# Correlation products on 8 x 16 pixel tiles instead of 4 x 32 row strips, with a re-laid copy of the stationary operand

## The chip, the cores and the metric

The kernel runs on one core of one Trainium2 chip. The metric is the device time of one execution in microseconds (us), which covers the profiled span and a little around it. Lower is better.

## The reference

Input is `x` of shape 8 x 512 x 32 x 32 in float32. Two layers follow each other, each `x = x + conv(group_norm(x))`. What is inside `conv`, cut to its core:

```python
norm = sqrt(sum(feature * feature, axis=1));  fn = feature / max(norm, 1e-12)
fp = pad(fn, 2 pixels on each side of h and w)
for cc in range(5):
    for r in range(5):
        sims.append(sum(fp[:, :, r:h + r, cc:w + cc] * fn, axis=1))   # 25 correlation maps
out = relu(einsum('bihw,oi->bohw', concat([feature, vol]), conv_w) + conv_b)
```

So each pixel needs the dot product over 512 channels of its own vector with those of its 5 x 5 neighbours, scaled by the two norms, and then a 1 x 1 convolution from 512 + 25 to 512 channels.

## The kernel before

The work is cut into 16 *units*, one for each layer and image, in teams of four images: units 0 to 3 are layer 0 of images 0 to 3, units 4 to 7 are layer 1 of the same images, and so on. A unit is 512 channels (4 tiles `t` of 128 partitions) by 1024 pixels.

- **Normalising.** VectorE reads each tile for its statistics (L759) and closes them (`stats_done`, last instruction L772). TensorE averages over groups with one small matmul (`average`, L461), VectorE forms scale and offset (`unit_affine`, L778 to L802), and ScalarE writes the normalised tile as float16 high part (`norm_tile`, L627) and twice the float32 value (`double_tile`, L633, GpSimd L432 for units 0 to 2). VectorE's `low_tile` (L808) forms the float16 low part from both. `opnd` holds high and low parts of four units in a ring.
- **Correlation products** (`product`, L470). The pixels are cut into 8 blocks of 4 rows x 32 columns (128 pixels). For each block the stationary operand is the high part of its 128 pixels, and the moving operand is the block's rows with two rows more above and below: 8 x 32 = 256 columns, or 6 x 32 = 192 for the first and last block. There are two moving parts (high, low) and four channel tiles, so a unit has 8 x 4 x 2 = 64 such matmuls. A pair of blocks fills one PSUM bank. There are four pairs `p`; pair `p` waits until ScalarE has copied pair `p - 2` out (`band_out_of_psum`, L643).
- **Skewing.** SyncE writes `band` to DRAM (L340) and reads it back along a diagonal into `skew` (L346), so that each pixel has its neighbours at fixed places. VectorE scales them (`neighbours`, L832 to L852), TensorE transposes them (`turn`, L520), ScalarE copies them to `rows` (L654), and SyncE writes them out (L356, L358). They come back as shifted views: issued by GpSimd (`views_from_dram`, L267 to L277), by SyncE in units 0 and 1. VectorE forms the 25 maps (`correlation`, L817 to L825), and GpSimd's DMAs bring them into `vol` (`volume_in`, L286).
- **Convolution.** A unit has 8 groups (4 output tiles x 2 pixel halves). Each is 12 matmuls of 512 columns (`channels`, L530) and one with `vol` (`volume`, L539). ScalarE applies relu (`rectified`, L662), VectorE adds into `x` (`added`, L886).

The order on every engine is written by hand. Units 0 to 2 have their own start-up sequence. From `k = 3` on there are equal *slots*: in slot `k` TensorE runs `products(k, 0..3)` with `average(k + 1)` between pair 1 and pair 2, then groups 4 to 7 of unit `k - 2`, groups 0 and 1 of unit `k - 1`, `turn(k)`, and groups 2 and 3 of unit `k - 1`. VectorE does in slot `k`: `unit_affine(k + 1)`, `correlation(k - 1)`, `low_tile(k + 1, 0)` and `(.., 1)`, `added` of group 4, `low_tile(.., 2)`, `added`, `neighbours(k)`, `low_tile(.., 3)`, and then additions and statistics of unit `k + 2`. Slot 4 also turns the weights of layer 1 (L510, L874).

## Time and profile before

| | |
|---|---|
| median of 3 runs | 540.35 us (539.79 to 542.28) |
| profiled execution | 540.12 us |
| its span | 538.4 us |
| TensorE matmul busy | 490.8 us, 91% |
| VectorE busy | 350.5 us, 65% |
| ScalarE busy | 278.6 us, 52% |
| GpSimd busy | 131.8 us, 24% |

The span is what the profiler records from the first to the last instruction; the profiled execution's own time is 1.7 us longer. TensorE's share covers work with different limits: in the start-up TensorE waits for the other engines, later it does not. So the stretches have to be read apart.

### The profile page before, as it was taken

The numbers are of one execution on the slowest core, as the hardware profiler recorded it, in microseconds if no ns is written. First come the engines' busy times: TensorE is split into PE (matmuls) and PEld (weight loads), VectorE is DVE, ScalarE is ACT, GpSimd is POOL, SyncE is SP. The second block draws the span as 40 slices with busy tenths as digits, with TensorE's granted clock in tenths as the row PEclk, the third lists the DMA queues.
The fourth block names the chain that finished last, engine by engine and source line by source line (L and its number), as shares of the span: only waits on it lengthen the run. The fifth ranks groups of instructions, "written<-read, shape, count | busy, mean of one in ns | idle before, by whom it ended". The sixth has DMA issues, their size and how long they took to land.

```text
span 538.4 us, 7705 instructions
## 1 busy us (share of the span) xinstructions
PE 490.8 (91%) x2824; PEld 278.2 (52%) x2824; DVE 350.5 (65%) x820; ACT 278.6 (52%) x370; POOL 131.8 (24%) x189
## 2 busy tenths in 40 slices
PE   0658699489998999999999999999999999999996
PEld 0535355354644646464645556464646455564442
DVE  4788794767869296958758595858677676433322
ACT  1352544575394656647393757556473938433222
POOL 3453511040521313131220404040313112040400
PEclk9989799789999999999999999999999999999999
DMA  8282444441332716494957625042332326362332
GB/s 295 99 270 67 129 165 133 133 134 38 94 92 74 219 49 211 149 309 131 321 165 254 212 102 161 15 129 47 98 89 75 110 79 185 138 203 90 126 126 114
DMA packets 58547, 75.81 MB, mean 141 GB/s; under 512 B 11764, under 2 KB 45612, under 8 KB 58510
## 3 DMA queue, kind: packets, MB, share of 16 engines
q1 hardware_dynamic: 48718, 66.40, 36.7%
q0 software_dynamic: 9792, 8.92, 7.0%
q8 instruction: 22, 0.36, 0.3%
q14 instruction: 15, 0.12, 0.1%
HBM read 34.97 MB, written 37.79 MB: 135 GB/s over the span
## 4 chain that ended last, share of the span: by engine, by line
PE 77%; DVE 10%; ACT 4%; DMA 4%; POOL 2%; SPq 2%; issue 2%; DVEq 0%; ACTq 0%
PE conv_ps L530 56%; PE gram_ps L470 14%; PE conv_ps L539 5%; DVE stats L759 3%; POOL v L432 2%; DVE opnd L808 2%; DMA xs<-in_x_dram 1%; ACT opnd L627 1%; PE turn_ps L520 1%; ACT v L633 1%; DVE wmax L858 1%; ACT act_out L662 1%; DMA skew<-band_dram 1%; DMA band_dram<-band 1%; DVE xs L886 1%
## 5 line engine op out<-in xcount | busy, mean ns | idle before, releaser
L530 PE MATMUL conv_ps<-opnd,wh 128*128 128x512 f16 x512 | 194.9, 381 | 1.2 <-DVE wl L874 1.2
L530 PE MATMUL conv_ps<-opnd,whh 128*128 128x512 f16 x512 | 194.7, 380 | 0.0
L530 PE MATMUL conv_ps<-opnd,wl 128*128 128x512 f16 x512 | 194.7, 380 | 0.0
L662 ACT ACTIVATE act_out<-conv_ps,bias,wdown 128x512 f32<-128x512 f32 x128 | 96.4, 775 | 141.0 <-PE conv_ps L539 129.1
L886 DVE TENSOR_TENSOR xs<-xs,act_out 128x512 f32<-128x512 f32 x128 | 87.7, 696 | 50.8 <-ACT act_out L662 50.2
L470 PE MATMUL gram_ps<-opnd 128*128 128x256 f16 (+1 forms) x960 | 105.0, 269 | 3.4 <-ACT band L643 3.4
L470 PEld LDWEIGHTS gram_ps<-opnd 128*128 128x128 f16 x960 | 91.1, 100 | 16.6 <-ACT band L643 3.7
L808 DVE SCALAR_TENSOR_TENSOR opnd<-opnd,v 128x1024 f16<-128x1024 f16 x64 | 78.4, 1235 | 28.7 <-ACT v L633 21.3
L627 ACT ACTIVATE opnd<-xs,affine 128x1024 f16<-128x1024 f32 x64 | 78.8, 1238 | 17.4 <-DVE affine L802 17.4
L759 DVE BATCH_NORM_STATS2 stats<-xs 128x6 f32<-128x512 f32 x128 | 79.9, 681 | 5.6 <-DMA xs<-in_x_dram 5.6
L530 PEld LDWEIGHTS conv_ps<-opnd,whh 128*128 128x128 f16 x512 | 50.0, 98 | 61.2 <-issue 1.0
L530 PEld LDWEIGHTS conv_ps<-opnd,wh 128*128 128x128 f16 x512 | 50.2, 98 | 58.8 <-POOL whh L424 1.3
L530 PEld LDWEIGHTS conv_ps<-opnd,wl 128*128 128x128 f16 x512 | 50.2, 98 | 57.5 <-issue 0.8
L633 ACT ACTIVATE v<-xs,affine 128x1024 f32<-128x1024 f32 x52 | 64.4, 1238 | 6.1 <-DVE opnd L808 6.1
L267 POOL DMA_DIRECT2D mirror<-rows_dram x14 | 9.5, 678 | 232.0 <-DMA rows_dram<-rows 232.0
L286 POOL DMA_DIRECT2D vol<-corr_h x48 | 33.2, 697 | 105.7 <-DVE corr_h L825 105.6
L539 PE MATMUL conv_ps<-vol,wvol 96*128 96x512 f16 x128 | 47.2, 396 | 11.7 <-DMA vol<-corr_h 11.7
L643 ACT ACTIVATE band<-gram_ps 128x448 f32<-128x448 f32 (+1 forms) x60 | 32.5, 560 | 20.2 <-PE gram_ps L470 20.2
L817 DVE TENSOR_TENSOR mirror<-mirror,rn_own 100x256 f32<-100x256 f32 x16 | 6.8, 424 | 49.1 <-DMA rn_far<-rows_dram 49.1
L277 POOL DMA_DIRECT2D rn_far<-rows_dram x56 | 34.1, 744 | 0.0
L539 PEld LDWEIGHTS conv_ps<-vol,wvol 96*128 96x128 f16 x128 | 12.6, 100 | 27.6 <-DMA vol<-corr_h 12.3
L432 POOL TENSOR_SCALAR v<-xs,affine 128x1024 f32<-128x1024 f32 x12 | 21.7, 1817 | 18.5 <-DVE affine L802 11.8
(77 smaller groups left out, 238.6 us busy)
## 6 DMA issues: line engine op xcount, KB each, us to landing
xs<-in_x_dram SPq DMA_DIRECT2D x32, 512.0 KB, 6.4
band_dram<-band SPq DMA_DIRECT2D x64, 256.0 KB, 2.9
out_dram<-xs SPq DMA_DIRECT2D x32, 512.0 KB, 2.9
skew<-band_dram SPq DMA_DIRECT2D x32, 266.0 KB, 3.5
vol<-corr_h POOLq DMA_DIRECT2D x48, 50.0 KB, 2.7
rows_dram<-rows SPq DMA_DIRECT2D x32, 65.8 KB
rows_dram<-rows SPq DMA_DIRECT2D x32, 63.3 KB
mirror<-rows_dram POOLq DMA_DIRECT2D x14, 110.9 KB, 2.6
```

Source lines behind the costliest of these rows:

```text
L277: eng.dma_start(rn_far[c:QPARTS:QUARTERS, 0:run], bass.AP(rows_dram, rn_row + c * QRUN, [[1, S], [PW, S], [1, run]])).then_inc(arrived, 16)
L286: eng.dma_start(vol[at:at + NS, k % 2, :].rearrange("s (q n) -> s q n", q=QUARTERS), corr_h[:, part, :]).then_inc(vol_in, 16)
L470: return pe.matmul(gram_at(u, p)[:, at:at + (r1 - r0) * WI], opnd[:, u % RING, 0, t, j * P:(j + 1) * P], opnd[:, u % RING, part, t, r0 * W ...
L530: pe.matmul(conv_ps[:, g % 4, :], w[:, l, t, m * P:(m + 1) * P], opnd[:, u % RING, part, t, n * HALF:(n + 1) * HALF], start=(t == 0 and w ...
L539: pe.matmul(conv_ps[:, g % 4, :], wvol[0:96, l, m * P:(m + 1) * P], vol[0:96, u % 2, n * HALF:(n + 1) * HALF], start=False, stop=True).the ...
L627: act.activation(opnd[:, u % RING, 0, t, :], xs[:, ring_slot(unit_batch(u)), t, :], ACT.Identity, bias=affine[:, 0, 1, t:t + 1], scale=aff ...
L633: act.activation(v2[:, t % 2, :], xs[:, ring_slot(unit_batch(u)), t, :], ACT.Identity, bias=affine[:, 1, 1, t:t + 1], scale=affine[:, 1, 0 ...
L643: act.activation(band[:, p, a:z], gram_at(u, p)[:, a:z], ACT.Copy).then_inc(band_sb, 1)
L662: act.activation(act_out[:, g % 2, :], conv_ps[:, g % 4, :], ACT.Relu, bias=bias[:, l, m:m + 1], scale=wdown[:, l, m:m + 1]).then_inc(relu, 1)
L759: last = dve.bn_stats(stats[:, t, h, :], xs[:, ring_slot(b), t, h * HALF:(h + 1) * HALF])
L808: dve.scalar_tensor_tensor(out=opnd[:, u % RING, 1, t, :], in0=opnd[:, u % RING, 0, t, :], scalar=-2.0, in1=v2[:, t % 2, :], op0=ALU.mult, ...
L886: dve.tensor_tensor(xt, xt, act_out[:, g % 2, :], ALU.add).then_inc(x_sum, 1)
```

## The change

The pixels are cut into 8 tiles of 8 rows x 16 columns (still 128 pixels). With the border of two pixels a tile needs 12 x 20 neighbours. Of these only what lies inside the image is computed: 18 of the 20 columns (`HELD = TC + R`), and 12 rows, or 10 for the top and bottom tiles. The moving operand is therefore 12 x 18 = 216 or 10 x 18 = 180 columns, read as runs of 18 elements out of rows of 32. [...] `strips` has room for one unit only: a copy waits until all products of the unit before are done. ScalarE's copy out of PSUM, the DRAM layout of `band` and the diagonal read follow the new tile shape (the read takes runs of 85 elements in place of 133). `turn` writes each transposed tile to its place in the image, as 8 runs of 16 columns in PSUM. Four small DMAs at the start (`pads`) go, and the clearing of `band` on GpSimd grows from 2 x 64 to 1920 columns. In the slots VectorE's order changes: `low_tile` and `strip_tile` of tiles 0 and 1 come ahead of `correlation(k - 1)`.

```diff
+    TR, TC = 8, 16
+    DOWN, ACROSS = HI // TR, WI // TC
+    BR, BC = TR + 2 * R, TC + 2 * R
+    BAND = BR * BC
+    HELD = TC + R
+        strips = sb("strips", [P, KT, ACROSS, HI * TC], F16)
...
-            def product(u, j, t, part):
-                return pe.matmul(gram_at(u, p)[:, at:at + (r1 - r0) * WI],
-                                 opnd[:, u % RING, 0, t, j * P:(j + 1) * P],
-                                 opnd[:, u % RING, part, t, r0 * WI:r1 * WI],
+            def product(u, p, c, t, part):
+                r0, r1 = held_rows(p)
+                c0 = 0 if c == 0 else WI - HELD
+                at = c * HALF // 2
+                return pe.matmul(gram_at(u, p)[:, at:at + HELD * (r1 - r0)],
+                                 strips[:, t, c, p * P:(p + 1) * P],
+                                 image(opnd[:, u % RING, part, t, :])[:, r0:r1, c0:c0 + HELD],
...
                 if p == 0:
                     pe.wait_ge(high, KT * (u + 1))
                     pe.wait_ge(low, KT * (u + 1))
+                    pe.wait_ge(stripped, KT * (u + 1))
...
+            def strip_tile(u, t):
+                wait(dve, gram, PAIRS * u)
+                dve.wait_ge(high, KT * u + t + 1)
+                dve.tensor_copy(strips[:, t, :, :].rearrange("p c (h w) -> p c h w", w=TC),
+                                opnd[:, u % RING, 0, t, :].rearrange("p (h c w) -> p c h w", c=ACROSS, w=TC)
+                                ).then_inc(stripped, 1)
...
             for t in range(KT):
+                strip_tile(0, t)
                 low_tile(0, t)
...
                 low_tile(3, 3)
+            for t in range(KT):
+                strip_tile(3, t)
...
             for k in range(STEADY, SLOTS):
+                if valid(k + 1):
+                    for t in range(2):
+                        low_tile(k + 1, t)
+                        strip_tile(k + 1, t)
                 if valid(k - 1):
                     correlation(k - 1)
-                if valid(k + 1):
-                    low_tile(k + 1, 0)
-                    low_tile(k + 1, 1)
...
+                        for t in {1: (2,), 3: (3,)}.get(j, ()):
+                            strip_tile(k + 1, t)
...
-                    last = pe.transpose(turn_ps[0:H_PART + NROWS, 0, i * P:(i + 1) * P],
+                    at = i % ACROSS * TC
+                    last = pe.transpose(image(turn_ps[0:H_PART + NROWS, 0, :])[:, i // ACROSS * TR:(i // ACROSS + 1) * TR,
+                                                                              at:at + TC],
```

TensorE, the products of one unit in a slot, before (rows of 128 stationary columns by so many moving columns; L461 is `average`):

```order
L470 MATMUL gram_ps<-opnd 128x192 x8
L470 MATMUL gram_ps<-opnd 128x256 x24
L461 MATMUL turn_ps<-mv,avg 128x8
L470 MATMUL gram_ps<-opnd 128x256 x24
L470 MATMUL gram_ps<-opnd 128x192 x8
```

And after, at the same place:

```order
L469 MATMUL gram_ps<-opnd,strips 128x180 x16
L469 MATMUL gram_ps<-opnd,strips 128x216 x16
L461 MATMUL turn_ps<-mv,avg 128x8
L469 MATMUL gram_ps<-opnd,strips 128x216 x16
L469 MATMUL gram_ps<-opnd,strips 128x180 x16
```

The number of matmuls is the same, 64; each streams fewer columns.

VectorE, a slot from the end of `unit_affine` to the start of `neighbours`, before (L817 to L825 are `correlation`, L808 is `low_tile`, L886 `added`):

```order
L802 TENSOR_SCALAR affine<-affine 128x8
L817 TENSOR_TENSOR mirror<-mirror,rn_own 100x8x32
L818 TENSOR_TENSOR own<-own,rn_far 100x8x32
L820 TENSOR_TENSOR corr<-own,mirror 100x256
L823 TENSOR_SCALAR corr_h<-corr 100x256
L825 SCALAR_TENSOR_TENSOR corr_h<-corr,corr_h 100x256
L808 SCALAR_TENSOR_TENSOR opnd<-opnd,v 128x1024 x2
L886 TENSOR_TENSOR xs<-xs,act_out 128x512
L808 SCALAR_TENSOR_TENSOR opnd<-opnd,v 128x1024
L886 TENSOR_TENSOR xs<-xs,act_out 128x512
L832 TENSOR_SCALAR nsq<-skew 128x8
```

And after (L832 to L840 are now `correlation`, L815 `low_tile`, L901 `added`, L822 the new copy):

```order
L815 SCALAR_TENSOR_TENSOR opnd<-opnd,v 128x1024
L822 COPY strips<-opnd 128x1024
L815 SCALAR_TENSOR_TENSOR opnd<-opnd,v 128x1024
L822 COPY strips<-opnd 128x1024
L832 TENSOR_TENSOR mirror<-mirror,rn_own 100x8x32
L833 TENSOR_TENSOR own<-own,rn_far 100x8x32
L835 TENSOR_TENSOR corr<-own,mirror 100x256
L838 TENSOR_SCALAR corr_h<-corr 100x256
L840 SCALAR_TENSOR_TENSOR corr_h<-corr,corr_h 100x256
L901 TENSOR_TENSOR xs<-xs,act_out 128x512
L815 SCALAR_TENSOR_TENSOR opnd<-opnd,v 128x1024
L822 COPY strips<-opnd 128x1024
```

`correlation` has moved behind two `low_tile` and two copies, and three copies stand ahead of `neighbours`. The fourth copy comes after `low_tile(.., 3)`.

## Rows read from the trace of the kernel before

**Rows 1.** The page: busy us, share of the span and instructions of each engine.

```profile
PE 490.8 (91%) x2824; PEld 278.2 (52%) x2824; DVE 350.5 (65%) x820; ACT 278.6 (52%) x370; POOL 131.8 (24%) x189
```

**Rows 2.** Busy time by stretch: start-up, slots 3 and 4, the rest.

```profile
core 0: us, PE busy (x) PEld busy (x) DVE busy (x) ACT busy (x) POOL busy (x), PEclk, DMA share, GB/s
61.77:110.59 48.82, 39.44 (x216) 22.38 (x216) 36.23 (x80) 25.23 (x33) 9.30 (x8) 0.87 0.45 139
110.59:163.38 52.79, 49.61 (x278) 27.88 (x279) 38.66 (x89) 32.31 (x42) 17.03 (x25) 0.97 0.32 90
163.38:538.40 375.02, 370.32 (x2124) 204.85 (x2124) 231.34 (x547) 200.26 (x265) 77.42 (x122) 1.00 0.45 143
```

**Rows 3.** One slot, same columns.

```profile
322.25:351.86 29.61, 29.61 (x175) 16.75 (x174) 21.85 (x57) 17.61 (x23) 6.35 (x10) 1.00 0.30 84
```

**Rows 4.** Products of one unit alone (L470): 8 of 192 columns, 24 of 256.

```profile
322.25:322.91 0.66, 0.66 (x9) 0.66 (x8) 1.00 0.00 0
322.91:325.53 2.62, 2.62 (x26) 2.24 (x24) 1.00 0.41 82
```

**Rows 5.** TensorE's timeline: start us, us, engine, line, operation.

```profile
11.78 0.57 PE L461 MATMUL turn_ps<-mv,avg 128*128 128x8 f32 x2 [11.78 <-DVE mv L772]
...
101.84 1.89 PE L539 MATMUL conv_ps<-vol,wvol 96*128 96x512 f16 x4 [7.00 <-DMA vol<-corr_h]
...
110.59 5.12 PE L470 MATMUL gram_ps<-opnd 128*128 128x256 f16 x32 [2.19 <-ACT band L643]
...
163.38 0.63 PE L510 MATMUL gram_ps<-ident,xs 128*128 128x128 f32 x4 [2.01 <-DVE wl L874]
...
325.53 0.29 PE L461 MATMUL turn_ps<-mv,avg 128*128 128x8 f32 x2
...
345.37 0.60 PE L539 MATMUL conv_ps<-vol,wvol 96*128 96x512 f16 x2
345.80 0.60 PE L520 MATMUL turn_ps<-ident,nbr 128*115 128x128 f32 x4
```

**Rows 6.** VectorE groups by form: mean ns of one behind the busy time.

```profile
L808 DVE SCALAR_TENSOR_TENSOR opnd<-opnd,v 128x1024 f16<-128x1024 f16 x64 | 78.4, 1235 | 28.7 <-ACT v L633 21.3 <-POOL v L432 7.2
...
L817 DVE TENSOR_TENSOR mirror<-mirror,rn_own 100x256 f32<-100x256 f32 x16 | 6.8, 424 | 49.1 <-DMA rn_far<-rows_dram 49.1
...
L823 DVE TENSOR_SCALAR corr_h<-corr 100x256 f16<-100x256 f32 x16 | 4.7, 294 | 0.6
...
L886 DVE TENSOR_TENSOR xs<-xs,act_out 128x512 f32<-128x512 f32 x128 | 87.7, 696 | 50.8 <-ACT act_out L662 50.2
```

**Rows 7.** VectorE's timeline in the slot from 322.25.

```profile
329.32 0.43 DVE L817 TENSOR_TENSOR mirror<-mirror,rn_own 100x256 f32<-100x256 f32 x1 [1.06 <-DMA rn_far<-rows_dram]
...
330.90 0.43 DVE L825 SCALAR_TENSOR_TENSOR corr_h<-corr,corr_h 100x256 f16<-100x256 f32 x1
...
333.95 1.22 DVE L808 SCALAR_TENSOR_TENSOR opnd<-opnd,v 128x1024 f16<-128x1024 f16 x1 [1.04 <-ACT v L633]
...
338.76 0.17 DVE L832 TENSOR_SCALAR nsq<-skew 128x8 f32<-128x8 f32 x1
339.85 0.20 DVE L835 RECIPROCAL rn<-nrm 128x8 f32<-128x8 f32 x1 [0.91 <-ACT nrm L648]
...
341.72 1.21 DVE L808 SCALAR_TENSOR_TENSOR opnd<-opnd,v 128x1024 f16<-128x1024 f16 x1
...
351.44 0.16 DVE L772 TENSOR_TENSOR mv<-mv,gtmp 128x4 f32<-128x4 f32 x1
```

**Rows 8.** VectorE's and ScalarE's timeline at unit 3.

```profile
101.06 1.23 DVE L808 SCALAR_TENSOR_TENSOR opnd<-opnd,v 128x1024 f16<-128x1024 f16 x1 [1.04 <-ACT v L633]
102.20 4.84 DVE L759 BATCH_NORM_STATS2 stats<-xs 128x6 f32<-128x512 f32 x8
...
108.66 1.45 ACT L662 ACTIVATE act_out<-conv_ps,bias,wdown 128x512 f32<-128x512 f32 x2 [3.43 <-DVE xs L886]
```

**Rows 9.** The page: DMA issues (times issued, KB each, median us to landing).

```profile
vol<-corr_h POOLq DMA_DIRECT2D x48, 50.0 KB, 2.7
```

More of the change, by code:

```diff
@@ L479, in first_products @@
                     pe.wait_ge(high, t + 1)
+                    pe.wait_ge(stripped, t + 1)
                     pe.wait_ge(low, t + 1)
                     for p in range(PAIRS):
-                        for j in (2 * p, 2 * p + 1):
+                        for c in range(ACROSS):
                             for part in range(2):
-                                last = product(0, j, t, part)
+                                last = product(0, p, c, t, part)
                         if t == KT - 1:
@@ L492, in products @@
                     pe.wait_ge(low, KT * (u + 1))
+                    pe.wait_ge(stripped, KT * (u + 1))
                 pe.wait_ge(band_sb, PAIRS * u + p - 1)
-                for j in (2 * p, 2 * p + 1):
+                for c in range(ACROSS):
                     for t in range(KT):
                         for part in range(2):
-                            last = product(u, j, t, part)
+                            last = product(u, p, c, t, part)
                 last.then_inc(gram, 1)
```

71 lines of the change are left out of this document (35 added, 36 removed).

## The prediction, written before the changed kernel ran

> **What bounds the kernel now.** First the page's head: TensorE is busy for 490.8 of 538.4 us [rows 1]. That share hides two regimes, so I read the busy time by stretch next. From 163.38 us to the end TensorE is busy for 370.3 of 375.0 us [rows 2], and in a slot for all 29.61 us, with VectorE at 21.9 and ScalarE at 17.6 [rows 3]. There a microsecond less of matmuls is a microsecond less of time, as long as no other engine's order becomes longer than the slot. Before that TensorE has holes. Its timeline shows which waits end last: the first statistics at 11.78, `vol` of unit 1 at 101.84 (7.00 us of waiting), ScalarE's `band` at 110.59 (2.19), VectorE's `wl` at 163.38 (2.01) [rows 5]. Ahead of each of these VectorE, ScalarE and SyncE set the pace, and shorter products only make the hole longer.
>
> **The products.** A unit has 48 matmuls of 256 columns and 16 of 192. The distance from start to start is what counts: the first eight take 0.66 us, 82.5 ns each for 192 columns; the next 24 take 2.62 us, 109.2 ns each for 256 [rows 4]. That is 0.417 ns a column plus 2.5 ns, at full granted clock. After, a unit has 32 of 216 and 32 of 180. By that line they take 92.5 and 77.5 ns. Sum: 6.56 us before, 32 x 92.5 + 32 x 77.5 = 5.44 after, so 1.12 us less per unit. Two reservations. The shortest distance that the trace shows is 82.5 ns, and there the weight loads already fill the time (0.66 of 0.66 us); if that is a floor, the saving is 0.96. And the moving operand is now read in runs of 18 elements, which no row shows; a read that is no slower costs nothing, and one at half speed would add 5.4 us per unit. I take 1.12: VectorE reads runs of 32 out of rows of 36 (L817, `mirror`, 424 ns for 256 elements) at the rate at which it reads whole runs (L886: 696 ns for 512, so 1.06 ns an element and 152 ns fixed, which gives 424 for 256) [rows 6], so breaks between runs alone cost nothing there. Units 5 to 15, eleven of them, lie wholly where TensorE is the bound: 11 x 1.12 = 12.3 us. For units 0, 1, 2 and 4 the shorter products end in front of a wait, so I count nothing. Of unit 3 the second half (5.12 us for 32 matmuls after the wait at 110.59, partly at the low clock: the stretch has 0.87 on average before it [rows 2, 5]) shrinks by a sixth, 0.8 us.
>
> **The copy.** Four per unit, 64 in all, 1024 float16 elements. No row shows one. Bounds: `low_tile` handles 1024 elements with two inputs in 1235 ns. `corr_h` (L823), one input, takes 294 ns for 256: with 152 fixed that is 0.555 ns an element, about half of the two-input form's 1.06, and by it the copy takes 720 ns. That row reads four bytes an element and the copy two; if speed goes by bytes it is 152 + 0.277 x 1024 = 436 ns, the low end [rows 6]. I take 0.44 us, since both sides of the copy are half as wide and its runs of 16 are even. The Trainium skill, "VectorE: DVE Perf Modes", section on the perf-mode tier table, says a one-input copy with 16-bit data on both sides in SBUF runs four elements at a time, and with mixed or 32-bit data two; L823 at half the cost per element of L817 agrees with the second half, and no row shows the first. The sum does not use it.
>
> **A slot after the change.** Times from the slot's start T (322.25 before). `average` came at T + 3.28 [rows 5]; it comes at T + 2.72 now, 0.56 earlier, and ScalarE's chain of norm and double tiles with it. `low_tile(.., 1)` started at T + 11.70, when ScalarE's `v` landed [rows 7], so now at 11.14; the first copy fits in the hole of 1.04 us ahead of it. It ends at 12.36, the second copy at 12.8, `correlation` (329.32 to 331.33, 2.0 us) at 14.8 [rows 7]. It used to lie in a hole of VectorE that ScalarE left; now it does not. Then addition, low tile, addition (0.70, 1.23, 0.70 by their rows [rows 6], less some overlap between neighbours) to 17.2, third copy 17.6. `neighbours` took 2.96 us (338.76 to 341.72) with 0.91 of waiting for ScalarE, which by then stands free: 2.4, so to 20.0. `turn` stands at T + 23.55 - 1.12 = 22.4 on TensorE [rows 5]: not late. Then the 9.88 us from the start of the last low tile (341.72) to the end of `stats_done` (351.60, L772) [rows 7] and the fourth copy in them: 20.0 + 9.88 + 0.44 = 30.3. The slot is now 28.49 long and the next `average` can run at 28.49 + 2.72 = 31.2. So 0.9 us are left, of 3.5 before (351.60 against 351.86 + 3.28 = 355.14). Three copies lie on this path; the point at which VectorE becomes the bound is 0.44 + 0.9 / 3 = 0.74 us for a copy. `vol` is the other queue that gets later: `correlation` ends at 14.8, GpSimd starts some 0.7 later, issues three DMAs of about 0.7 each, and the last lands 2.7 after [rows 9], so 20.3; the first `volume` stood at T + 23.1 [rows 5] and stands at 22.0: 1.7 us are left of some 9.
>
> **Start-up.** GpSimd's longer clearing and the `pads` that go lie under the first load and its statistics, for which TensorE waits until 11.78 [rows 5]: nothing. Units 0 and 1: the copy ahead of `low_tile(u, 0)` is not covered, the other three fall into waits for GpSimd's `v`: 2 x 0.4. Unit 2: three copies in a dense stretch make `average(3)` some 2 us late, but the chain of SyncE's issues (views, band, skew) from `turn(1)` on ends only some 0.5 us later, so I estimate that 0.5 of all this remain at the last low tile of unit 3. Unit 3: all four copies stand between that tile (101.06) and the statistics (102.20), whose end frees the additions, on which ScalarE waits for 3.43 us (108.66) [rows 8], then `band`, then TensorE (110.59) [rows 5]: 4 x 0.44 = 1.8 on the path. Together +2.2 at 110.59, minus the 0.8 above: +1.4 at the start of slot 4. Slot 4: TensorE waits for `wl`, behind `neighbours` in VectorE's order. By the walk above, with statistics of the slot's own (scaling of layer 1's maxima ahead), `correlation` and copies leave `wl` 1.3 later. +2.7 at 163.38.
>
> **The sum.** 540.1 (the profiled execution, which is 0.2 under the median of 540.35) + 2.7 - 12.3 = 530.5; I say 531. ScalarE's copies are shorter (432 or 360 columns for 512 or 448) and the diagonal read carries less, in shorter pieces: beside other work, nothing, within 0.5 us either way in the start-up.
>
> **Rivals.**
> (A, forecast) 531, own range 527 to 535: the floor of 82.5 ns takes 1.8 off, a copy of 0.72 us adds 4 x 0.28 + 3 x 0.28 = 2.0 in the start-up and nothing in slots, and a start-up kinder than I walked it gives 2.7 back.
> (B) One of the thin margins in the slot breaks (0.9 us to `average`, 1.7 to `vol`), or `turn` gets slower: 0.5 us in each of 11 slots, 536. For it: both margins are estimates, and slots with image loads have slower landings (the trace's `vol` at 101.84 came late). Against: the margins are positive in every slot that I walked. A rule speaks for the `turn` part: four transposes stand 0.11 us apart, 0.44 together, and were they to take double, 11 x 0.44 = 4.8 would give 535. The Trainium skill, "PSUM — Partial Sum Buffer", section on the specifications, says any non-contiguous pattern in PSUM slows matmuls significantly; the trace has no such write, and the runs are of 16 float32.
> (C) The copy runs at one element a cycle, like `low_tile`, 1.23 us. The slot's VectorE path grows by 3 x 0.8 = 2.4 us and passes the margin by 1.5 (it decides from 0.74 us a copy), and the slot becomes 28.49 + 1.5 = 30.0 in place of 29.61: 11 x 0.4 = 4 to 5 more than before, and the start-up costs 2.7 + 7 x 0.8 = 8.3, with some 2 for unit 2. 540 + 5 + 10 = 555 or so. Slower than before. Against: L823 is faster than that per element already.
> (D) Broken runs slow the moving operand. A unit reads 16 x 44 = 704 runs; at 1.12 / 704 = 1.6 ns a run (four columns' time) the gain is gone, and at half speed it is 540.1 + 2.7 + 11 x (5.4 - 1.1) = 590. Slower too. Nothing in the trace shows it on TensorE.
> (E) No change, 538 to 542: any of these by half.
>
> **Chances.** A 0.65, B 0.13, C 0.08, D 0.08, E 0.06. What a measurement can tell from no change is about 0.5%, 2.7 us. Faster: A and most of B, 0.75. Same: E and the rest of B, 0.09. Slower: C and D, 0.16. Range 526 to 541: C and D stay outside, with 0.03 below.
>
> **What would show it.** Products: 216-column matmuls 92.5 ns apart, a unit in 5.44 us, slots of 28.5 us with TensorE busy throughout. Copy: L822 at 0.42 to 0.46 us. The end of `stats_done` some 0.9 us ahead of `average`, no wait of TensorE at L461 in the slots. `vol` landing ahead of the volume matmul. Start-up: the wait for `band` ends at about 112.8, the one for `wl` at about 166. Wrong it would be if the product distance doesn't follow the columns, or if TensorE waits at L461, at the volume or at `turn` in each slot.

## The result, and the profile after

| | before | after |
|---|---|---|
| time, median | 539.99 us (538.54 to 542.28) | 544.19 us (540.38 to 547.7) |
| profiled execution | 540.12 us, span 538.4 | 546.94 us, span 545.2 |
| TensorE busy | 490.8 us, 91% | 485.6 us, 89% |
| VectorE busy | 350.5 us, 65% | 373.2 us, 68% |

The changed kernel takes 1.0073 times as long, 95% interval 1.0055 to 1.0091. The prediction said 531, in a range of 526 to 541, and gave 0.16 to slower. It was wrong, in the sign too. In the comparisons by stretch below the profiled execution of the kernel after is one of its longer ones (546.94 us in a spread of 540.38 to 547.7), so what it loses is somewhat more than the medians' 4.2 us.

One word on what is new on VectorE, since its times are read below: the copy `strip_tile` (L822) lays the high part of one channel tile into `strips`, first the left half of the image and then the right one, so that the 128 pixels of a tile lie together.

First the busy time by stretch, cut where TensorE's waits end, as [rows 2] were (the row of 391.85 is one late slot, for [rows 3]); columns as there.

```profile
core 0: us, PE busy (x) PEld busy (x) DVE busy (x) ACT busy (x) POOL busy (x), PEclk, DMA share, GB/s
64.08:117.21 53.13, 40.03 (x217) 22.92 (x217) 37.49 (x87) 24.61 (x33) 9.89 (x12) 0.82 0.42 126
117.21:169.72 52.51, 48.02 (x278) 27.41 (x279) 40.45 (x96) 32.04 (x42) 13.60 (x19) 0.96 0.27 72
169.72:302.71 132.99, 129.54 (x752) 71.47 (x753) 95.17 (x229) 74.56 (x100) 27.71 (x42) 0.98 0.51 166
302.71:545.20 242.49, 235.57 (x1373) 128.63 (x1371) 150.14 (x360) 122.94 (x165) 52.17 (x80) 1.00 0.38 118
391.85:420.61 28.76, 28.76 (x175) 16.25 (x174) 22.07 (x55) 17.40 (x23) 6.59 (x10) 1.00 0.28 77
```

The late slot does what was forecast: 28.76 us against 29.61, TensorE busy all through. The loss lies ahead of such slots. The end of the start-up came at 163.38 [rows 5] and comes at 169.72, 6.3 us later. By comparing the starts of equal slots: slot 5 begins 9.3 us later than before, slot 10 (322.25 in [rows 3]) 11.35 later at 333.60, the last one 7.8 later (478.14 for 470.35). So everything up to slot 5 cost 9.3 us, the five slots in the middle 2 more in place of gaining, and only the slots after that gained. Of the 9.3, 3.0 lie behind the end of the wait, and they are the granted clock: from there to slot 5 TensorE has no further wait, and the same work takes 13.49 us at a mean granted clock of 0.78, where the kernel before took 10.52 (163.38 to 173.90) at 1.00.

```profile
169.72:183.21 13.49, 13.48 (x56) 6.64 (x57) 9.94 (x18) 4.74 (x8) 1.25 (x2) 0.78 0.13 45
```

The products follow the columns. TensorE's timeline of the late slot (start, duration, engine, line, operation) shows the 64 products of the unit. Each row of 32 names only its first form; it holds 16 of 180 and 16 of 216 columns, in the order shown with the change:

```profile
391.85 2.92 PE L469 MATMUL gram_ps<-opnd,strips 128*128 128x180 f16 x32
394.61 0.30 PE L461 MATMUL turn_ps<-mv,avg 128*128 128x8 f32 x2
394.76 3.10 PE L469 MATMUL gram_ps<-opnd,strips 128*128 128x216 f16 x32
397.70 0.38 PE L533 MATMUL conv_ps<-opnd,wh 128*128 128x512 f16 x1
```

From start to start they are about 79 and 93.5 ns apart (77.5 and 92.5 forecast). The convolution follows at 397.70, 5.85 us after the first product.

The waits of SyncE, by line: in total, times, longest. First before, then after.

```profile
SPq L346 <- DMA band_dram<-band: 38.1, 16, 3.6
```

```profile
SPq L358 <- ACT rows L661: 100.7, 12, 12.6
SPq L342 <- ACT band L650: 98.2, 41, 17.6
SPq L325 <- DVE xs L901: 95.8, 24, 8.3
SPq L348 <- DMA band_dram<-band: 79.4, 16, 8.1
```

SyncE waits 79.4 us, in place of 38.1, until the bands have landed in DRAM, ahead of the diagonal read. What that does is seen at unit 2, before and then after (SyncE's issues of a line, with the time that they take):

```profile
87.24 2.13 SPq L340 DMA_DIRECT2D band_dram<-band  x4
92.06 0.91 SPq L346 DMA_DIRECT2D skew<-band_dram  x2
```

```profile
89.64 3.11 SPq L342 DMA_DIRECT2D band_dram<-band  x4
98.01 0.94 SPq L348 DMA_DIRECT2D skew<-band_dram  x2
```

The writes are issued 2.4 us later than before and the read 5.95 us later. TensorE's timeline shows the rest of the path: `turn` waits for `neighbours`, then the products for a copy, which stands behind these in VectorE's order, then the second half of the products for `band`.

```profile
103.84 1.20 PE L522 MATMUL turn_ps<-ident,nbr 128*115 128x128 f32 x4 [3.22 <-DVE nbr L867]
109.22 5.34 PE L469 MATMUL gram_ps<-opnd,strips 128*128 128x180 f16 x32 [4.18 <-DVE strips L822]
117.21 4.56 PE L469 MATMUL gram_ps<-opnd,strips 128*128 128x216 f16 x32 [2.12 <-ACT band L650]
```

The page's count of packets (the single pieces in which the DMA engines move data), which the first experiment gives its meaning:

```profile
DMA packets 49836, 71.62 MB, mean 131 GB/s; under 512 B 27628, under 2 KB 36900, under 8 KB 49798
```

### The profile page after: what moved, and what is told of

It is laid out like the page before. It is cut to its first block, busy times and chain, and to the rows that moved or that the text cites. A ratio compares the mean times of both kernels' runs of the same rounds, so it can differ in the third digit from the quotient of the medians.

```text
span 545.2 us, 7837 instructions
## 1 busy us (share of the span) xinstructions
PE 485.6 (89%) x2824; PEld 274.2 (50%) x2824; DVE 373.2 (68%) x884; ACT 274.5 (50%) x370; POOL 135.6 (25%) x188
## 2 busy tenths in 40 slices
DMA packets 49836, 71.62 MB, mean 131 GB/s; under 512 B 27628, under 2 KB 36900, under 8 KB 49798
## 4 chain that ended last, share of the span: by engine, by line
PE 45%; DVE 23%; DMA 16%; POOL 5%; ACT 4%; issue 4%; SPq 2%; DVEq 0%; ACTq 0%
PE conv_ps L533 34%; PE gram_ps L469 7%; DVE stats L766 5%; DMA rows_dram<-rows 4%; DMA rn_far<-rows_dram 4%; DVE opnd L815 4%; DVE xs L901 4%; PE conv_ps L542 3%; DMA band_dram<-band 2%; DMA out_dram<-xs 2%; POOL v L432 2%; DVE strips L822 2%; ACT opnd L630 1%; DMA skew<-band_dram 1%; ACT v L636 1%
## 5 line engine op out<-in xcount | busy, mean ns | idle before, releaser
L815 DVE SCALAR_TENSOR_TENSOR opnd<-opnd,v 128x1024 f16<-128x1024 f16 x64 | 78.9, 1233 | 55.8 <-ACT v L636 53.8
L901 DVE TENSOR_TENSOR xs<-xs,act_out 128x512 f32<-128x512 f32 x128 | 87.2, 686 | 36.0 <-ACT act_out L669 35.4
L469 PE MATMUL gram_ps<-opnd,strips 128*128 128x180 f16 (+1 forms) x960 | 93.4, 254 | 8.0 <-DVE strips L822 4.2
L469 PEld LDWEIGHTS gram_ps<-opnd,strips 128*128 128x128 f16 x960 | 85.6, 100 | 15.5 <-ACT band L650 6.9
L295 POOL DMA_DIRECT2D vol<-corr_h x48 | 35.4, 745 | 160.0 <-DVE corr_h L840 159.9
L542 PE MATMUL conv_ps<-vol,wvol 96*128 96x512 f16 x128 | 46.4, 389 | 11.7 <-DMA vol<-corr_h 11.7
L650 ACT ACTIVATE band<-gram_ps 128x360 f32<-128x360 f32 (+1 forms) x60 | 28.5, 493 | 15.8 <-PE gram_ps L469 15.8
L822 DVE COPY strips<-opnd 128x1024 f16<-128x1024 f16 x64 | 30.2, 475 | 3.2 <-ACT opnd L630 3.2
L542 PEld LDWEIGHTS conv_ps<-vol,wvol 96*128 96x128 f16 x128 | 12.2, 99 | 28.3 <-DMA vol<-corr_h 14.0
L432 POOL TENSOR_SCALAR v<-xs,affine 128x1024 f32<-128x1024 f32 x12 | 21.7, 1810 | 18.3 <-DVE affine L809 9.2
```

The source lines that it names most:

```text
L295: eng.dma_start(vol[at:at + NS, k % 2, :].rearrange("s (q n) -> s q n", q=QUARTERS), corr_h[:, part, :]).then_inc(vol_in, 16)
L469: return pe.matmul(gram_at(u, p)[:, at:at + HELD * (r1 - r0)], strips[:, t, c, p * P:(p + 1) * P], image(opnd[:, u % RING, part, t, :])[:, ...
L542: pe.matmul(conv_ps[:, g % 4, :], wvol[0:96, l, m * P:(m + 1) * P], vol[0:96, u % 2, n * HALF:(n + 1) * HALF], start=False, stop=True).the ...
L815: dve.scalar_tensor_tensor(out=opnd[:, u % RING, 1, t, :], in0=opnd[:, u % RING, 0, t, :], scalar=-2.0, in1=v2[:, t % 2, :], op0=ALU.mult, ...
L822: dve.tensor_copy(strips[:, t, :, :].rearrange("p c (h w) -> p c h w", w=TC), opnd[:, u % RING, 0, t, :].rearrange("p (h c w) -> p c h w", ...
L901: dve.tensor_tensor(xt, xt, act_out[:, g % 2, :], ALU.add).then_inc(x_sum, 1)
```

## The experiments

Two theories after the result. W: the band is written with a destination of 8 rows by 16 pixels, this form lands late, and all that follows in SyncE's and VectorE's order is late with it. V: the copies and the new order of VectorE's work (correlation behind two low tiles and copies) make additions, views and outputs late. "Changed" is the kernel after, 544.19 us.

**1. The write in one even step.**

```
-    HL_PITCH = TC * (WL_PITCH + 1) - BC
+    HL_PITCH = TC * WL_PITCH
...
-                                  [[HL_PITCH, TR], [WL_PITCH, TC], [1, ACROSS * BAND]])
+                                  [[WL_PITCH, P], [1, ACROSS * BAND]])
```

(and a floor of 1.0e7 in `nsq`, so that nothing overflows: the neighbours are those of wrong pixels here). Expected:

> The changed kernel with the band written to DRAM at one constant pitch over its 128 pixels (one outer dimension of 128 where it had 8 x 16), same 128 runs of 1920 bytes and the same read. Left out: the neighbours are then those of wrong pixels for all but the first image row of a tile, and the floor under the squared length is raised so that nothing overflows; no instruction goes. Theory W (the write in 8 x 16 form lands late: SyncE waited 79.4 us for it where it was 38.1 before): the wait of SyncE for the band falls to about 40 us, the skew of unit 2 lands 2 to 3 us earlier, time 538 to 541. Theory V (VectorE's longer and reordered path makes additions, output DMAs and views late): the wait for the band may fall, the time stays at 543 to 545.

Measured: 531.98 us (531.01 to 535.77), 0.9859 of before (0.9833 to 0.9885). That is 6 us faster than even theory W had it (538 to 541). SyncE's wait is back, and so are the landings; the page's packets beside them:

```profile
SPq L348 <- DMA band_dram<-band: 40.0, 16, 4.2
```

```profile
DMA packets 50348, 71.62 MB, mean 135 GB/s; under 512 B 28140, under 2 KB 37412, under 8 KB 50310
...
band_dram<-band SPq DMA_DIRECT2D x64, 240.0 KB, 2.9
```

The destinations differ by 4 floats a row of 16 pixels, the bytes are the same, and the even form has 512 packets more, 8 for each of the 64 writes. They are small ones (28140 against 27628 under 512 B; of 4 bytes 7247 against 6735). The times of the single packets say the same: of the band's packets of 1920 bytes at most 11 overlapped at any time in the kernel after, with 8 at once for longer than any other number, and up to 22 with the even write, most often 16 when they were many. So the 8-row form ran on 8 of the 16 DMA engines. The Trainium skill, "DMA: Bandwidth & Descriptors", section "Why a DMA increments its semaphore by 16 and not by 1", has the rule: the number of engines is the largest one up to 16 that divides the outermost dimension on both sides; 8 here, and 16 with 128 outside. The packet counts agree: the section lets each engine in use post an end of its own, which makes 8 fewer for each write.

At unit 2 the diagonal read now follows as before:

```profile
87.60 1.92 SPq L342 DMA_DIRECT2D band_dram<-band  x4
92.65 0.92 SPq L348 DMA_DIRECT2D skew<-band_dram  x2
```

and the first stretch of full rate begins at 164.56, 1.2 us later than before. W holds, and the whole 12 us between the two kernels are in this form of the write.

**2. The correlation back ahead of the low tiles and copies.**

```
                     unit_affine(k + 1)
+                if valid(k - 1):
+                    correlation(k - 1)
                 if valid(k + 1):
                     for t in range(2):
                         low_tile(k + 1, t)
                         strip_tile(k + 1, t)
-                if valid(k - 1):
-                    correlation(k - 1)
```

> The changed kernel with correlation(k - 1) put back ahead of the two low tiles in the slots; copies stay behind the low tiles. Theory V, order part: slots in which nothing lands late get as long as TensorE's work (28.5 to 28.8), the additions of unit k - 2 come about 2 us earlier in each slot, the middle slots lose their waits, 539 to 541. Theory W: no change, 543 to 545. A third possibility: in slots whose views land late the low tiles now wait behind them, and it gets slower, 546.

Measured: 558.22 us (556.97 to 559.15), 14.0 more than changed; ratio 1.0332 (1.031 to 1.0354). Theory V had 539 to 541, W no change; the third possibility named was right in kind (slower, for the low tiles then wait behind the views) but had it at 546. TensorE waits ahead of `turn` 13.3 us (6.8 in the kernel after) and for ScalarE's `act_out` 6.5. In a slot from 283 on, VectorE stands 11.77 us before the correlation, with the low tiles and copies queued behind it:

```profile
295.14 0.42 DVE L832 TENSOR_TENSOR mirror<-mirror,rn_own 100x256 f32<-100x256 f32 x1 [11.77 <-DMA rn_far<-rows_dram]
```

Against V's half on the order: it is what kept the late band from costing more.

**3. Copies alone, in the kernel before.** Four idle copies a unit at the places of the changed kernel, old order and old products:

```
+            def strip_tile(u, t):
+                dve.wait_ge(high, KT * u + t + 1)
+                dve.tensor_copy(strips[:, t, :, :].rearrange("p c (h w) -> p c h w", w=16),
+                                opnd[:, u % RING, 0, t, :].rearrange("p (h c w) -> p c h w", c=2, w=16))
```

> The kernel before with the four copies per unit added on VectorE at the changed kernel's places, into a buffer that nobody reads; products, DMAs and the order of correlation as before. Theory V: the copies alone cost 3 us or more, 543 to 545 (my walk had 4 x 0.44 at unit 3, 0.5 ahead of it and 1.3 in slot 4, of which 0.9 are copies: 3.2). Theory W: under 2 us, since the start-up hides them behind SyncE's chain.

Measured: 544.80 us (543.91 to 548.89), ratio 1.0087 (1.0068 to 1.0107). 4.8 us for 64 copies, with the correlation in its old place: V's range, and over the 2 us that W allowed, so here V was right about the copies. In the profiled execution, the longest of the seven (548.89), slot 5 begins 3.1 us later than before, and slots 5, 9 and 10 take 2.9, 1.6 and 0.6 us more than the 29.61 of a late one, with TensorE waiting for `neighbours` and statistics. In the old order the copies cost in slots too.

**4. The 8-row form in the kernel before.**

```
-                                  [[BAND, P], [P * BAND, 2], [1, BAND]])
+                                  [[16 * BAND, 8], [BAND, 16], [P * BAND, 2], [1, BAND]])
```

> The kernel before with the destination pattern of the band write in 8 x 16 form in place of 128, same addresses and the same 256 runs of 1024 bytes. Theory W: the write lands about 2.5 us later each time (SyncE's wait for it 38 to about 80 us), the chain of unit 2 lengthens by as much, 542 to 544. If instead the far spread of the runs in DRAM makes the changed kernel's write slow: no difference, 540.

Measured: 539.82 us, ratio 0.9996 (0.9979 to 1.0012), SyncE's wait 39.2. Inconclusive on W: here 8 steps of 16 pixels are one even step again, and the trace has as many 4-byte packets (7251) as the kernel before, and as many of the band's packets at once (22, 23 before), so the write never was on 8 engines. The rival in the text above, the wide spread of the changed kernel's runs in DRAM, falls by experiment 1, whose runs lie as far apart.

**5. The even write, without the copies.**

```
-                                  strips[:, t, c, p * P:(p + 1) * P],
+                                  opnd[:, u % RING, 0, t, (2 * p + c) * P:(2 * p + c + 1) * P],
...
-                dve.tensor_copy(strips[:, t, :, :]...
+                return
```

> The changed kernel with the band written in one even step over 128 partitions (as in the earlier run of that kind), and now also without the copies of the high parts: the products take blocks of 128 pixels that lie together in the operand as the stationary side. It leaves the copies out, and the products and what follows are of the wrong pixels. Against the 531.98 us of the run with the even write alone it gives the price of the copies. The prediction put them at 0.44 us a tile on VectorE: 4 tiles of unit 3 on the way to the first full-rate slot, 1.8 us, and 1.3 us in slot 4, nothing later. Theory W: the copies cost what was predicted, 2 to 4 us, so 528 to 530 us. Theory V: they also cost in the middle slots, where VectorE is the engine that is late, as four idle copies a unit did in the kernel before (4.8 us), so 525 to 527.5 us. If they are wholly covered: 531 to 532.5.

Measured: 527.76 us (525.99 to 528.27), ratio 0.9767 (0.9746 to 0.9788). The copies cost 4.2 us, between the two theories' ranges; the forecast's terms for them are 1.8 at unit 3 and 1.3 in slot 4, 3.1 together. TensorE's wait for `wl` ends at 160.26 in place of 164.56: all 4.3 us are in the start-up, nothing in the slots after (the last slot begins at 458.44 in place of 462.72).

**6. The even write, with the correlation first.** Edit 1 and edit 2 together.

> The changed kernel with the band written in one even step over 128 partitions, and the correlation of the unit before moved back ahead of the low tiles and the copies of a slot, where the kernel before had it. The products then wait for copies that come at the end of a slot's work on VectorE. Its neighbours are of the wrong pixels, as in the earlier run with the even write. With the late write the same move cost 14 us (558.22 against 544.19). If the cost is that the copies come late for the products whatever the write does: 540 to 548 us. If it came only together with the late band: 531 to 535 us. If the old order is better once the band lands in time: 526 to 530 us.

Measured: 539.36 us (538.01 to 541.33), ratio 0.9991 (0.9976 to 1.0007), just under the first of the three ranges. The old order costs 7.4 us also with a band that lands in time, and 14.0 with the late one. The waits are not for the copies, as that text had it: from 176 us on TensorE waits ahead of `turn` (3.2 us) and `average` (2.7), in slots 5, 6, 8, 9 and 10. So once the copies are there the new order is worth something by itself, and the late band doubles it.

**7. Tiles of 16 rows by 8 columns.** A kernel that computes everything and whose write has 16 outer steps. Pairs are the two edge tiles or the two middle tiles of a half.

```
-    TR, TC = 8, 16
+    TR, TC = 16, 8
+    COLS = (0, 3, 1, 2)
...
+            c = COLS[2 * (p % 2) + s]
+            return c, max(c * TC - R, 0), min((c + 1) * TC + R, WI)
...
-                                 strips[:, t, c, p * P:(p + 1) * P],
+                                 strips[:, t, c, p // 2 * P:(p // 2 + 1) * P],
```

> The changed kernel with its tiles turned: 16 rows by 8 columns in place of 8 rows by 16, so the tiles are again 128 pixels, the products again 180 and 216 columns, and the copy is the same in size (4 column strips of 8 in place of 2 of 16). A pair of tiles is now (left edge, right edge) or (the two in the middle) of one half of the image. The write of the correlation bands has 16 outer steps in place of 8, one for each of the 16 DMA engines; everything is computed as in the reference. Theory W (the 8-step write uses 8 of the 16 DMA engines, lands late, and costs the 12 us between the changed kernel and the forecast): the write lands in about 3 us, SyncE waits for it about 40 us in all (79.4 in the changed kernel), and the time is 530 to 534 us. Theory V (the copies and the order of VectorE's work delay the slots): they are unchanged here, so 542 to 546 us. A third outcome, 534 to 541, would mean that the turned tiles cost something of their own (copy in shorter runs, turn in 16 runs of 8 columns).

Measured: 547.11 us (546.47 to 549.14), ratio 1.0138 (1.0115 to 1.016). None of the three: the write lands in 3.1 us and SyncE waits 40.2, as W has it, but the time is above V's. The groups by shape tell why (mean ns behind the busy time):

```profile
L475 PE MATMUL gram_ps<-opnd,strips 128*128 128x216 f16 x480 | 68.2, 301 | 4.2 <-ACT band L657 4.2
...
L475 PE MATMUL gram_ps<-opnd,strips 128*128 128x180 f16 x480 | 46.3, 252 | 3.4 <-ACT band L657 2.1 <-DVE strips L829 1.3
```

In experiment 1 the same two groups stood at 51.5 and 46.4 us. The edge tiles' products (180 columns, runs of 10) keep 79 ns from start to start, the middle ones (216 columns, runs of 12) take 127 in place of 93.5. 32 a unit by 33.5 ns by 16 units is 17 us of TensorE's work. In time it is less, since the start-up hides its part: a slot takes 30.05 us in place of 28.95 in experiment 12, which differs in nothing else, and the medians are 12.6 apart. It is a small form of the forecast's rival D, which the kernel after did not show.

**8. The middle runs moved by 2 columns.** Columns 4 to 15 and 16 to 27 of a row in place of 6 to 17 and 14 to 25 (and the floor in `nsq`).

```
-            return c, max(c * TC - R, 0), min((c + 1) * TC + R, WI)
+            return c, *((0, TC + R) if c == 0 else (WI - TC - R, WI) if c == 3 else (4, 16) if c == 1 else (16, 28))
```

> The changed kernel with turned tiles (16 rows by 8 columns), and the moving side of the two middle tiles begun 2 columns to the side: columns 4 to 15 and 16 to 27 of each image row in place of 6 to 17 and 14 to 25. The number of columns, of runs (18) and their length (12 fp16) are the same; only the place of a run within the row's 64 bytes differs: 6 to 17 and 14 to 25 cross byte 32 of the row, 4 to 15 and 16 to 27 don't. The middle tiles' products are of the wrong pixels. In the turned kernel a product of a middle tile (216 columns) took 127 ns from start to start, one of an edge tile (180 columns in 18 runs of 10, none of which crosses byte 32) 79 ns. Theory X (each run costs once for every 32 bytes of the row that it touches: 36 pieces in 127 ns, 3.5 ns each, as long as that is above the column rate): with 18 pieces the middle products go back to the column rate, 93 to 94 ns, a unit to 5.5 to 5.8 us, and the kernel to 529 to 533 us. Theory Y (runs of 12 fp16 are slow as such): 127 ns and 546 to 548 us as before.

Measured: 535.05 us (533.81 to 537.08), ratio 0.9909 (0.9884 to 0.9934).

```profile
L475 PE MATMUL gram_ps<-opnd,strips 128*128 128x216 f16 x480 | 50.9, 260 | 4.1 <-ACT band L657 4.1
```

Distance 92.5 ns: the place of the run decides, not its length, against Y. The time is 2 us above X's range, so X was right on the products and not on the kernel.

**9. The edge runs moved over byte 32.** As 8, and `(8, 18)` and `(10, 20)` for the edge tiles.

> As the run with the middle tiles begun 2 columns to the side, and now the edge tiles' moving side too is moved: columns 8 to 17 and 10 to 19 in place of 0 to 9 and 22 to 31, so that their runs of 10 cross byte 32 of the row. The products are of the wrong pixels. Theory X (3.5 ns for every 32 bytes touched): edge products take 36 pieces, 127 ns in place of 79 (more than the longer middle products at 93 to 94), and the time is 545 to 549 us. Theory Y (the length of the runs decides): edge 79, middle 127, 546 to 548 us; so the two are told apart by which products are slow.

Measured: 534.73 us (one run). Edge products 78 ns, middle ones 92.5: neither is slow, and both ranges are missed. X with pieces of 32 bytes falls too.

**10. One write for each image row.**

```
+                    for r in range(TR):
+                        dst = bass.AP(band_dram, q * GSZ + p * ACROSS * BAND + r * HL_PITCH,
+                                      [[WL_PITCH, TC], [1, ACROSS * BAND]])
+                        sp.dma_start(dst, band[r * TC:(r + 1) * TC, p, :]).then_inc(band_out, 16)
```

> The changed kernel with each write of a band cut into 8 writes, one for each image row of the tile: 16 partitions, even steps, so every one can go over 16 DMA engines. 32 writes a unit in place of 4, all issued by SyncE; everything is computed as in the reference. Theory W (the write in 8 steps uses half of the DMA engines and lands late): each write lands in 2 to 3 us; the last pair's 8 issues of about 0.35 us put the end of the last one some 2.5 us behind the first, so SyncE waits for the landing 40 to 55 us in all, and the time is 532 to 538 us, if SyncE's 28 further issues a unit (about 10 us of a slot) hold nothing else up. If they do, 540 to 550. If the fan-out had nothing to do with it: 544 or more.

Measured: 609.92 us (609.63 to 611.53), ratio 1.1303 (1.1276 to 1.133).

```profile
SPq L349 <- DMA band_dram<-band: 21.3, 16, 1.7
```

```profile
310.01 16.84 SPq L343 DMA_DIRECT2D band_dram<-band  x32
328.12 0.93 SPq L349 DMA_DIRECT2D skew<-band_dram  x2
329.09 7.71 SPq L325 DMA_DIRECT2D out_dram<-xs  x2
```

That is 60 us above every range in the text. The landing is waited for only 1.7 us at most, but 32 issues fill 16.84 us of SyncE, one every 0.53 us (most take 0.42, two of them 0.95 and 1.62) and not the 0.35 expected, and the read is issued 21.3 us into the slot. TensorE waits 52.2 us in all ahead of `turn`. The wait became issues.

**11. Only the last pair's write cut in rows.**

> The changed kernel with only the last pair's band write of each unit cut into 8 writes by image row; the first three keep the 8-step form. Everything is computed as in the reference. Theory W: only the last write's landing is waited for, but the first three still queue on 8 of the engines ahead of it (each takes 16 packets of 98 ns on each of the 8, 1.6 us, and comes every 1.4 us), so the landing is earlier than in the changed kernel but later than with all cut: SyncE waits 50 to 65 us in all, and 534 to 541 us. If all that counts is SyncE's issues, this is better than the run with all cut; if all that counts is the engines, it is worse.

Measured: 544.65 us (543.03 to 547.1), ratio 1.0088 (1.0062 to 1.0114); SyncE waits 30.0 us. Both bounds missed: the wait was under 50, the time above 541.

```profile
274.00 5.06 SPq L343 DMA_DIRECT2D band_dram<-band  x3
279.10 4.09 SPq L348 DMA_DIRECT2D band_dram<-band  x8
287.36 0.94 SPq L354 DMA_DIRECT2D skew<-band_dram  x2
```

Eight issues take 4.1 us, and from the last one to the read it is still 4.2 us. The gain of the one is about the price of the other: SyncE's wait is 49.4 us less than in the kernel after, 3.1 a unit, and the seven further issues of 0.51 us are 3.6 a unit. Against 10 it says that SyncE's issues are what ruined that run.

**12. Tall tiles, the operand 2 elements further in memory.** Kernel 7, everything computed, with

```
-        opnd = sb("opnd", [P, RING, 2, KT, PIX], F16)
+        opnd_mem = sb("opnd", [P, RING * 2 * KT * PIX + 32], F16)
+        opnd = opnd_mem[:, 2:2 + RING * 2 * KT * PIX].rearrange("p (r a t n) -> p r a t n", r=RING, a=2, t=KT)
```

> The changed kernel with turned tiles (16 rows by 8 columns), and the operand tile placed 2 fp16 elements further in memory, so that the middle tiles' runs of 12 columns begin at bytes 16 and 32 of their 64-byte row and touch two pieces of 16 bytes (three of 8), in place of bytes 12 and 28 and three pieces (four of 8). Everything is computed as in the reference. The runs so far: runs of 12 beginning at bytes 12 and 28 took 127 ns a product, at bytes 8 and 32 92.5 ns, runs of 10 beginning at bytes 16 and 20 78 ns, so neither byte 32 nor the length alone decides. Theory Z (the count of aligned pieces a run touches decides): middle products 92 to 94 ns, the unit 5.8 to 6.0 us, and with the band write landing in 3 us 529 to 534 us: a correct kernel that is faster than both. If the shift costs the convolution's products something (their 512 columns then begin 4 bytes off), the mean of those rises from 381 ns: 5 ns more would be 8 us. If the slow products have another cause: 547 us.

Measured: 534.48 us (532.54 to 535.27) beside 539.21 of before on the same chip, ratio 0.9914 (0.9895 to 0.9934). It beats both kernels, the one before by 0.9%, and is 0.5 us above theory Z's range. The groups:

```profile
L539 PE MATMUL conv_ps<-opnd,wh 128*128 128x512 f16 x512 | 195.0, 381 | 0.4 <-DVE wl L897 0.4
...
L476 PE MATMUL gram_ps<-opnd,strips 128*128 128x216 f16 x480 | 52.4, 264 | 4.8 <-ACT band L658 4.8
```

Middle products 92.5 ns apart, and the convolution, whose runs now begin 4 bytes off, unchanged at 381 ns. A late slot:

```profile
376.97:405.92 28.95, 28.70 (x175) 16.17 (x174) 22.11 (x55) 17.41 (x23) 6.61 (x10) 1.00 0.27 72
```

It is 0.19 us longer than the one of the kernel after, with 0.25 us of waiting for `band` ahead of its last pair. That is 2 of the 2.5 us by which this kernel stays behind experiment 1.

**13. The same with 4 elements.**

> As the run with the operand 2 elements further, but 4 elements: the middle runs of 12 begin at bytes 20 and 36 of the row. They then touch two pieces of 16 bytes (16 to 47 and 32 to 63), but four pieces of 8 bytes (16 to 47 and 32 to 63). If pieces of 16 bytes count: 92 to 94 ns a product and the time of the other shift. If pieces of 8 bytes count, or the start has to be a multiple of 8 bytes: 127 ns and about 545 to 548 us.

Measured: 534.6 us (one run), middle products 92.4 ns apart. So pieces of 8 bytes, or a start on 8 bytes, are not it. Pieces of 16 bytes fit the forms that ran, with a short run in three of them as the slow one:

| run, in bytes of the 64-byte row | pieces of 16 bytes | ns a product |
|---|---|---|
| 10 columns, begun at 0 and 44 (experiments 7, 8), 16 and 20 (9), 4 and 48 (12), 8 and 52 (13) | 2 | 77 to 79 (18 runs) |
| 12 columns, begun at 8 and 32 (8), 16 and 32 (12), 20 and 36 (13) | 2 | 92.5 (18 runs) |
| 18 columns, begun at 0 and 28 (1) | 3 | 79 (10 runs), 93.5 (12 runs) |
| 12 columns, begun at 12 and 28 (7) | 3 | 127 (18 runs) |

A fixed price for each piece does not fit, though: 54 pieces in 127 ns are 2.35 ns each, and at that the 36 pieces of a 180-column product would take 85 ns, where they took 77 to 79. So the table tells which forms were slow, and by which mechanism stays open.

The Trainium skill, "SBUF — State Buffer", section "Door 1: The DMA port swizzle (why `[64,N]` ≈ `[32,N]`)", speaks of lines of 16 bytes, of two accesses that a line needs for full bandwidth, and of a penalty for each access that crosses to a new one. The lines agree. The two accesses don't, if an access is an element: a run of 12 in three lines has two elements at least in each, and is slow.

## Why the prediction was wrong, by its own steps

**The step that failed** is the sentence in the sum that let the DMAs go: "beside other work, nothing, within 0.5 us either way in the start-up", and with it, in the start-up, that "the chain of SyncE's issues (views, band, skew) from `turn(1)` on ends only some 0.5 us later". The diagonal read of unit 2 was issued 5.95 us later. With the even write it was issued 0.6 us later (92.65 against 92.06). So the walk along that chain was right for a write over 16 engines, and wrong for this one: I had read the diff's new destination for its bytes and its pieces, not for its outermost 8. I had named no rival for it either. B's two margins in the slot, to `average` and to `vol`, did break, in the middle slots, but as an effect of the late band: with the even write TensorE has no wait there. B priced them at 5.5 us over all slots, and not what the start-up loses.

**Where it was lost**, by the starts of the slots (the medians, 544.19 and 531.98, are 12.2 us apart, the two profiled executions, 546.94 and 531.42, 15.5):

| | before | after | with the even write |
|---|---|---|---|
| wait for `wl` ends | 163.38 | 169.72 | 164.56 |
| slot 5 | 173.90 | 183.21 | 175.08 |
| slot 10 | 322.25 | 333.60 | 318.90 |
| last slot | 470.35 | 478.14 | 462.72 |

By slot 5 the kernel after stands 8.1 us behind the one with the even write, by slot 10 14.7, at the last slot 15.4. So half was lost in the start-up, and nearly all the rest in the middle slots, where the output and loads of images share SyncE and the DMA engines. Of the 7.3 us lost between slot 5 and the last slot TensorE's waits are 5.5; the kernel with the even write and the kernel before have none between 176 us and 390. After:

```profile
PE conv_ps L542 <- DMA vol<-corr_h: 3.1, 2, 2.0
PE turn_ps L461 <- DVE mv L779: 2.1, 4, 0.9
PE turn_ps L522 <- DVE nbr L867: 0.3, 1, 0.3
```

Slot 8, after, and then with the even write:

```profile
275.36 4.80 SPq L342 DMA_DIRECT2D band_dram<-band  x4
288.40 0.93 SPq L348 DMA_DIRECT2D skew<-band_dram  x2
293.71 5.53 SPq L325 DMA_DIRECT2D out_dram<-xs  x2
```

```profile
263.50 5.89 SPq L342 DMA_DIRECT2D band_dram<-band  x4
273.32 0.93 SPq L348 DMA_DIRECT2D skew<-band_dram  x2
278.75 5.53 SPq L325 DMA_DIRECT2D out_dram<-xs  x2
```

From the last write's issue to the read it is 8.2 us against 3.9. The slots begin at 271.26 and 261.37, so the outputs go out 22.5 us into the one and 17.4 into the other. They stand behind the read in SyncE's order; the next loads, `rows` and with these the views stand behind them, and in this stretch (264 to 308 us) of the kernel after TensorE waits 2.0 us for `vol` and VectorE 4.6 for `rn_far`:

```profile
DVE mirror L832 <- DMA rn_far<-rows_dram: 4.6, 1, 4.6
```

In a late slot without image loads the same form has 4.0 us from issue to read (2.3 with the even write), and there nothing is late. That the image loads are what makes it 8.2 fits these two numbers and was not tried by itself; the four writes also follow each other faster in slot 8 (4.80 us for 6.46), and in unit 2 of the start-up, with 3.11 us for the four, it is 5.3. The lower granted clock (0.959 of the profiled execution, against 0.972 with the even write and 0.981 before) adds to the loss: behind the wait that ends at 169.72 twelve convolution matmuls take 0.62 or 0.63 us each, the duration at the lower of the two levels, in place of 0.38:

```profile
170.61 0.63 PE L533 MATMUL conv_ps<-opnd,wh 128*128 128x512 f16 x1
```

TensorE had waited 2.98 us just before. With the even write the same stretch, from the end of the wait to slot 5, takes 10.52 us as it did before, and 13.49 in the kernel after:

```profile
164.56:175.08 10.52, 10.52 (x57) 5.59 (x57) 9.94 (x18) 4.75 (x8) 1.25 (x2) 1.00 0.17 53
```

So 3.0 of the 8.1 us by slot 5 are clock and the other 5.1 waits and clock ahead of it, which were not separated.

**The products**: right in the distance (79 and 93.5 ns for 77.5 and 92.5), and a slot was mis-sized: it shrank by 0.85 us, not by 1.12. The distances make 5.5 us; `average` takes 0.15 between them and a pause of some 0.16 came ahead of pair 3, for a `band` that ScalarE writes in the slot's middle and that the shorter products now reach first. 11 slots by 0.27 are 3.0 us.

**The copy**: 0.42 us in the slots for 0.44. In the start-up four took 1.26 to 1.39 us, each of them during a `v` of GpSimd (L432), beside which other copies took 0.42; the mean over all is 0.475. All 64 cost 4.2 us (experiment 5) for 3.1, all of it in the start-up, as forecast. C falls: none of the copies in the slots takes 1.23 us.

**The slot's walk**: right where nothing lands late. In the late slot, T being its start at 391.85, `correlation` ends at T + 14.55 (14.8 forecast), `neighbours` at T + 19.7 (20.0), and `stats_done` 1.8 us ahead of the next `average` (0.9).

```profile
405.97 0.43 DVE L840 SCALAR_TENSOR_TENSOR corr_h<-corr,corr_h 100x256 f16<-100x256 f32 x1
...
410.64 0.93 DVE L867 TENSOR_TENSOR nbr<-skew,nbr 128x200 f32<-128x200 f32 x2
```

What I had not priced is what the new order is worth once the copies are there: 7.4 us (experiment 6). The sum took it for granted that the order costs nothing.

**The start-up**: +2.7 forecast, +1.2 with the even write, +6.3 as it ran. **The sum again**, with these sizes: 530.5 less 1.5 plus 3.0 is 532.0, and the kernel with the even write takes 531.98 (its profiled execution 531.42). That the two agree to the digit is luck. So one missing term, of 12.2 us, made the miss; two smaller errors, of 1.5 and 3.0, partly cancelled and would have left the forecast inside its range.

**B's rule on `turn`**: four transposes into runs of 16 float32 in PSUM take 0.60 us in the slot, as before [rows 5], mean 286 ns, and 282 with the even write, as in the kernel before. No slower write showed. **D**: not in the kernel after, where runs of 18 go at the rate of columns; in experiment 7 it did show, at 33.5 ns a product.

## What to carry to other kernels

Where a change gives a DMA a new access pattern, read its outermost dimension before its bytes: here 8 in place of 128 halved the engines, and on an in-order chain write, read, `neighbours` that cost 12 us of 540, more than the 8 that the change gains without it. A transfer that is "beside other work" has to be followed to the first instruction that waits for it and to all that is queued behind that. And the gain may be had by asking for the same tile in another shape: 16 rows by 8 columns, with its runs placed so that they touch few pieces of 16 bytes, takes 534.5 us for 539.2 of the kernel before, with everything computed.

## What the runs showed of the hardware that I had not expected

- A DRAM destination of 8 x 16 rows of 1920 bytes ran on 8 DMA engines: it had 8 end packets a write fewer than the even form, and at most 11 of its data packets overlapped, for 22 in the even form. And the read that waits for it was issued 8.2 us after the last write in a slot with image loads (3.9 with the even form), 4.0 us in a quiet slot (2.3). Four issues of it in a row took SyncE 3.11 us, four of the even form 1.92.
- A matmul's moving side read in runs of 12 fp16 took 92.5 ns for 216 columns where each run touches two 16-byte pieces, and 127 ns where it touches three. Runs of 18 in three pieces, and of 10 in two, took 0.43 to 0.44 ns a column, as a whole row's 0.43 did.
- SyncE issued writes of 16 partitions one every 0.53 us in a row of 32, most of them 0.42 us long.
- Patterns that look nested are not always so: `[[16 * BAND, 8], [BAND, 16]]` behaved as one step of 128: as many packets as before, and 539.82 us for 539.97.
